# Stacked q and k of groups 1 to 7 laid out by DMA through DRAM instead of by matmul, in a one-core attention and expert kernel

## The chip, the cores and the metric

One core of a Trainium2 chip (trn2) runs the program. The metric is the device time of one execution in microseconds (us). Engines are named as in the profile: PE is TensorE, PEld its weight load, DVE VectorE, ACT ScalarE, POOL GpSimd, and SP SyncE, which here only issues DMAs. SPq is SP's sequencer, where a DMA is issued.

## What is computed

Two sequences of 512 tokens with 128 features, 16 heads of 8 features. The reference, cut to what matters here:

```python
x = x + attn(cond(x, c, w_cond), w_qkv, w_out)
# attn: q, k, v per head (B=2, H=16, S=512, hd=8), rotary turn of q and k
scores = einsum('bhsd,bhtd->bhst', q, k) / sqrt(hd)      # causal
attn   = softmax(scores);  out = einsum('bhst,bhtd->bhsd', attn, v) @ w_out.T
x = x + ffn(cond2(x, ...))   # cond2: 2 shared and 8 routed experts; ffn: top 3 of 8 zones per sequence
```

The softmax subtracts each row's true maximum. All is in fp32, and the score products are made exact to fp32 level by splitting q and k into a high and a low part.

## The kernel before, in words

The 32 pairs of sequence and head are worked in 8 groups of 4 heads (`GROUPS` = 8, `NG` = 4 groups to a sequence, `HG` = 4 heads to a group). After the rotary turn, `qk_hi` and `qk_lo` hold the high and low parts of q (index 0) and k (index 1), with 128 partitions = 16 heads x 8 features. A group's score matmuls want another layout, `stacked[:, 2n + i, :]`: each of the 4 heads takes 32 partitions, made of four blocks of 8 rows. For q the blocks are (ones or maximum rows, hi, hi, lo), for k (ones, hi, lo, hi). One product of K = 32 rows then sums hi*hi + hi*lo + lo*hi.

Before, `stack(w)` builds this on PE: for each group and for q and k, one matmul of a 0/1 selection matrix `sel` with `qk_hi` and one with `qk_lo` (L1254, L1255), into a PSUM bank; ACT's `copy_stacked(w)` (L926 for q, L928 for k, which adds the ones rows as a bias) moves it to SBUF. Group 0 has its own first version in halves (`stack_half`, `place_q0`, `copy_k0`, `copy_q0`).

Then, for each group n:

- SP's `pad_q(n)` and `pad_k(n)` copy each head's 32 partitions from `stacked` into the zeroed buffers `q_pad` and `k_pad` (4 DMAs each), so that a matmul over 128 partitions sees one head alone. Two buffers of each are used in turn.
- `scores_for_max(n, u)`, 12 units (L1271): PE makes q x k for the maximum, in a ring of three PSUM banks. DVE's `reduce_max` (L617) masks and reduces each block. `place_max` (L630, L632) puts the negated maxima into `max_pad`, and `lay_max_under_q` (L1283, L1285) adds them to q's free rows; ACT copies the result (`copy_qm`, L945).
- `scores_for_exp(n, u)`, 6 units (L1302, L1305, L1306): PE makes k x q, in two pairs of PSUM banks used in turn (`ST_ORDER`), ACT takes the exponential (L939), POOL masks the diagonal (L515).
- `weigh_v` (L1322): PE multiplies with v; ACT copies out (L951); SP's `store_sums(n)` writes it to DRAM.

Each engine runs a fixed list; waits are semaphores. PE's list is the loop at the end of its block: in iteration n stand the exponential units of group n, the last three blocks of `weigh_v` of group n - 1, and the maximum units of groups n + 1 and n + 2 (they run 20 units ahead, `LEAD`). In iterations 0 to 4 the two `stack` calls of group n + 3 (`STACK_IN`) stand between `scores_for_exp(n, 3)` and `(n, 4)`, and take a turn in the banks of `ST_ORDER`. Groups 1 and 2 are stacked earlier, between the maximum units of group 0. The second sequence's q and k are projected in `project(0)` and `project(1)` and turned by POOL while group 0 runs.

Expert weights (`raw`, 1792 KB) are loaded in one DMA after group 0. ACT and POOL split them in seven chunks into high and low parts (`split_high`, `split_low`), at the places in `SPLITS`; chunk 4 and later overwrite `qk_hi` and `qk_lo`, so they wait for the last `stack`. `INV_AT` says behind which maximum units DVE inverts and normalises the first sequence's sums; for this, SP's `gather(0)` reads sums and outputs back from DRAM, and `spread_inverse(0)` writes and rereads the inverse.

After the attention come experts and zones, a loop that PE fills; nothing in it is touched.

Of the kernel before, what the change touches and what calls it, by code (L numbers as in the profile page):

```python
# [7 lines left out]
ACT = mybir.ActivationFunctionType  # L8
# [97 lines left out]
INV_AT = [78, 88]  # L106
SPLITS = {(2, 0): 0, (2, 2): 1, (3, 0): 2, (3, 2): 3, (4, 0): 4, (4, 2): 5, (5, 0): 6}
# [32 lines left out]
def program(nc, io, scratch, out):  # L140
# [9 lines left out]
    with ctx:  # L150
# [120 lines left out]
        def sum_of(i):  # L271
# [86 lines left out]
        def _(sp):  # L358
# [11 lines left out]
            def pad_q(n):  # L370

                s = n % 2
                sp.wait_ge(rep_copied, 3 if n == 1 else 2 * n + 3)
                if n >= 2:
                    sp.wait_ge(mx_full, (n - 1) * MXU)
                for j in range(HG):
                    q = slice(32 * j, 32 * j + 32)
                    sp.dma_start(f32_of(q_pad[s][q, j, :]), f32_of(stacked[q, 2 * n, :])).then_inc(q_padded[s], 16)

            def pad_k(n):  # L380

# [12 lines left out]

# [32 lines left out]
            pad_q(2)  # L427
# [33 lines left out]
        def _(pool):  # L461
# [5 lines left out]
            G.memset(f32_of(sel[:, 1, :, :]), 0.0).then_inc(sel_zero, 1)  # L467
# [5 lines left out]
            for g in range(2, NG):  # L473
                G.memset(f32_of(sel[:, g, :, :]), 0.0).then_inc(sel_zero, 1)
# [8 lines left out]
            def split_low(k):  # L483
# [3 lines left out]
                if k == UP_COLS // S:  # L487
                    pool.wait_ge(rep_ready, 2 * GROUPS + 2)
# [20 lines left out]
            for n in range(GROUPS):  # L509
                for c in range(3):  # L510
# [344 lines left out]
        def _(act):  # L855
# [797 lines left out]
```

## Time and profile before

| | |
|---|---|
| median of 3 runs | 205.31 us (204.97 to 205.75) |
| profiled execution | 205.4 us, of which the core's span is 203.7 us |
| PE busy | 187.9 us, 92% of the span |
| ACT busy | 147.7 us, 73% |
| DVE busy | 141.5 us, 69% |
| attention loop (first exponential unit to the last group's value matmuls) | about 29 to 107 us |
| DMA | 15.72 MB, mean 77 GB/s |

A busy share is an average over stages. What an edit is worth is read from the rows of its stage: which engine stood idle, and who released it.

### The profile page before, as it was taken

Reading aid. Unit: us, or ns where it says so; the run is one execution under the profiler, and the core shown is the slowest. Engines: PE = TensorE matmul, PEld = TensorE weight load, DVE = VectorE, ACT = ScalarE, POOL = GpSimd, SP = SyncE. Lnnn points to the kernel's source line nnn. Section 1 sums busy time; section 2 is a strip of 40 time slices with the busy share of each in tenths; the row PEclk is TensorE's granted clock in tenths of the full one; section 3 lists DMA queues with packets and bytes.
Section 4 is the critical chain, followed back from the end, with each engine's and each line's share of the span. In section 5 each row is a group of like instructions: output and inputs, shape, how many; then the busy total and the mean of one; then the engine's idle time right before and its main releaser. Section 6 shows DMA issues by size and latency. Waiting matters only on the chain.

```text
span 203.7 us, 3373 instructions
## 1 busy us (share of the span) xinstructions
PE 187.9 (92%) x1034; PEld 131.2 (64%) x1034; DVE 141.5 (69%) x459; ACT 147.7 (73%) x245; POOL 85.1 (42%) x100
## 2 busy tenths in 40 slices
PE   7994999999999997998999999999799989999993
PEld 3753766666666663664466776776557857788881
DVE  4584689888888885898027798468979845566552
ACT  4487848677878776879774485465688899899980
POOL 4616068461336363743332261021356962198000
PEclk9999799999999999999999999999999999999999
DMA  5602321229633233332111199600000000001001
GB/s 155 219 0 52 101 67 41 53 52 316 215 91 88 70 102 91 83 103 72 34 52 45 37 326 340 169 0 0 0 3 2 0 0 0 2 3 52 0 0 52
DMA packets 9509, 15.72 MB, mean 77 GB/s; under 512 B 2116, under 2 KB 3268, under 8 KB 9364
## 3 DMA queue, kind: packets, MB, share of 16 engines
q1 hardware_dynamic: 8916, 15.12, 24.5%
q10 hardware_dynamic: 576, 0.39, 0.6%
q8 instruction: 8, 0.13, 0.3%
q14 instruction: 9, 0.07, 0.1%
HBM read 9.16 MB, written 2.42 MB: 57 GB/s over the span
## 4 chain that ended last, share of the span: by engine, by line
PE 68%; DVE 15%; ACT 11%; issue 4%; POOL 1%; DVEq 0%; ACTq 0%; POOLq 0%
PE psum L1271 10%; PE psum L1400 9%; PE psum L1322 8%; PE psum L1402 8%; PE psum L1401 8%; PE psum L1302 6%; DVE psum L617 3%; PE psum L1305 2%; PE psum L1194 2%; PE psum L1254 2%; PE psum L1139 2%; DVE t_raw L763 2%; PE psum L1306 1%; ACT t_q_pad L991 1%; PE psum L1255 1%
## 5 line engine op out<-in xcount | busy, mean ns | idle before, releaser
L617 DVE CUSTOM_DVE_ANT_0 psum<-psum,t_causal 128x128 f32<-128x128 f32 (+3 forms) x128 | 59.5, 523 | 15.5 <-PE psum L1271 14.9
L939 ACT ACTIVATE t_probs<-psum 128x768 f32<-128x768 f32 (+1 forms) x48 | 41.3, 883 | 4.0 <-PE psum L1302 3.0
L1271 PE MATMUL psum<-t_stacked,t_q_pad 128*128 128x256 f32 (+2 forms) x128 | 36.9, 361 | 0.6 <-ACT t_q_pad L886 0.2
L515 POOL TENSOR_SCALAR_AFFINE_SELECT t_probs<-t_probs 128x512 f32<-128x512 f32 x32 | 20.0, 638 | 32.4 <-ACT t_probs L939 32.4
L1271 PEld LDWEIGHTS psum<-t_stacked,t_q_pad 128*128 128x128 f32 x128 | 22.0, 190 | 13.8 <-DVE t_row_max L617 9.8
L781 DVE SCALAR_TENSOR_TENSOR t_q_pad<-psum,t_zw_all,t_q_pad 128x512 fp32r<-128x512 f32 x24 | 17.9, 749 | 11.6 <-ACT t_q_pad L989 11.6
L975 ACT ACTIVATE t_raw<-psum 128x512 f32<-128x512 f32 x24 | 14.3, 595 | 10.4 <-PE psum L1446 7.7
L1322 PE MATMUL psum<-t_probs,t_v_all 128*32 128x512 f32 (+3 forms) x256 | 20.5, 439 | 0.0
L549 POOL TENSOR_TENSOR t_q_pad<-t_raw,t_q_pad 128x512 fp32r<-128x512 f32 x8 | 10.3, 1290 | 20.1 <-ACT t_q_pad L991 20.1
L1302 PE MATMUL psum<-t_q_mov,t_k_pad 128*128 128x512 f32 (+1 forms) x64 | 18.3, 371 | 0.2
L617 DVE DVE_READ_ACCUMULATOR2_ANT t_row_max<- 128x1 f32 x128 | 18.2, 142 | 0.0
L989 ACT ACTIVATE t_q_pad<-psum,t_zw_all 128x512 fp32r<-128x512 f32 x24 | 16.6, 690 | 1.9 <-PE psum L1402 1.5
L769 DVE TENSOR_TENSOR psum<-t_raw,psum 128x512 f32<-128x512 f32 x16 | 11.1, 692 | 7.8 <-ACT t_raw L975 7.8
L1400 PE MATMUL psum<-t_stacked,t_up_hi 128*128 128x512 f32 x32 | 14.0, 437 | 0.7 <-DVE t_q_pad L784 0.4
L975 ACT ACTIVATE psum<-psum 128x512 f32<-128x512 f32 x24 | 14.1, 586 | 0.3 <-PE psum L1402 0.3
L1401 PE MATMUL psum<-t_stacked,t_up_lo 128*128 128x512 f32 x32 | 12.6, 394 | 0.0
L1402 PE MATMUL psum<-t_stacked,t_up_hi 128*128 128x512 f32 x32 | 12.6, 393 | 0.0
L1302 PEld LDWEIGHTS psum<-t_q_mov,t_k_pad 128*128 128x128 f32 x64 | 11.2, 189 | 1.8 <-ACT t_probs L939 0.7
L784 DVE TENSOR_TENSOR t_q_pad<-psum,t_q_pad 128x512 fp32r<-128x512 f32 x16 | 10.9, 684 | 2.0 <-ACT t_q_pad L991 1.6
L1322 PEld LDWEIGHTS psum<-t_probs,t_v_all 128*32 128x32 f32 x256 | 6.6, 109 | 8.4 <-issue 3.9
L1305 PE MATMUL psum<-t_q_mov,t_k_pad 128*128 128x256 f32 x32 | 9.1, 307 | 2.0 <-ACT t_probs L939 2.0
L945 ACT CAST t_q_mov<-psum 128x512 fp32r<-128x512 f32 x8 | 4.7, 586 | 8.0 <-PE psum L1285 8.0
(236 smaller groups left out, 420.9 us busy)
## 6 DMA issues: line engine op xcount, KB each, us to landing
t_k_pad<-t_stacked SPq DMA_DIRECT2D x32, 64.0 KB, 2.0
t_probs<-in_L_ffn_Wa SPq DMA_DIRECT2D x2, 1024.0 KB, 8.7
t_q_pad<-t_stacked SPq DMA_DIRECT2D x28, 64.0 KB, 2.0
scratch<-t_o_sb SPq DMA_DIRECT2D x7, 256.0 KB, 2.0
t_raw<-in_experts SPq DMA_DIRECT2D x1, 1792.0 KB, 7.6
t_raw<-in_rotary SPq DMA_DIRECT2D x2, 256.0 KB, 4.9
out_dram<-t_probs SPq DMA_DIRECT2D x2, 256.0 KB, 2.0
t_raw<-in_w_all ACTq DMA_DIRECT2D x2, 128.0 KB, 3.0
```

The lines of the kernel that those rows point to most:

```text
L515: last = G.affine_select(out=tri, in_=tri, compare_op=ALU.is_ge, fill=0.0, base=0, pattern=[[0, HG], [1, P]], channel_multiplier=-1)
L617: last = V.tensor_tensor_reduce(scores, scores, causal[:, S - width:S], 1.0, 3 * BIG, ALU.add, ALU.max, row_max[s][:, qb, j:j + 1])
L781: V.scalar_tensor_tensor(h_lo[r], hidden_of(i), weight_of(i), f32_of(h_hi[r]), ALU.mult, ALU.subtract).then_inc(lo_done, 1)
L939: A.activation(probs[s][:, c, 2 * h2:2 * h2 + 2, 0:w], ST[:, slot_of("exp", n, u):slot_of("exp", n, u) + 2, 0:w], ACT.Exp, scale=float(1.0 ...
L975: A.activation(o, pair_of(i)[:, 0, :], func, scale=scale).then_inc(act_done, 1)
L989: A.activation(h_hi[r], hidden_of(i), ACT.Identity, scale=weight_of(i)).then_inc(hi_done, 1)
L1271: last = T.matmul(ring("max", n, u)[:, i * 2 * P:i * 2 * P + width], q_pad[s][:, j, qb * P:(qb + 1) * P], stacked[:, 2 * n + 1, 0:width], ...
L1302: last = T.matmul(bank[:, 0:S - c * P], k_pad[s][:, j, c * P:(c + 1) * P], q[:, c * P:S], start=True, stop=True)
L1322: last = T.matmul(PV[32 * j:32 * j + 32, lo:hi], v_all[:, v0:v0 + 32], probs[n % 2][:, c, j, o:o + hi - lo], start=(kb == 0 and lo == 0), ...
L1400: T.matmul(o, hi, x_hi, start=start, stop=False)
L1401: T.matmul(o, lo, x_hi, start=False, stop=False)
L1402: return T.matmul(o, hi, x_lo, start=False, stop=stop)
```

## The change

Groups 1 to 7 are no longer stacked by `stack` and `copy_stacked`; both functions go, with three of the four selection matrices. Instead SP writes the rows of `qk_hi` and `qk_lo` to a DRAM area that has the stacked layout (`spill`: per sequence and per q or k, three DMAs: hi twice, lo once), fills in the ones and zero rows once from an input (`spill_rest`), and reads whole groups back into `stacked` (`load_stacked`). `pad_q` (groups 1 to 7) and `pad_k` read that DRAM area as well, not `stacked`. The two bank pairs of `ST_ORDER` carry only projections and exponential units. `raw` is loaded in seven DMAs, spread over iterations 1 to 4. The chunks are split one iteration later, and DVE's inversion and normalisation stand 2 and 5 maximum units later.

```diff
-STACK_IN = {0: 3, 1: 4, 2: 5, 3: 6, 4: 7}
-ST_ORDER = [("stack", 2), ("project", 1)]
+BY_PE = 1
+SPILLS = 3
+ST_ORDER = [("project", 0), ("project", 1)]
 for _n in range(GROUPS):
-    ST_ORDER += [("exp", _n, _u) for _u in range(4)] + ([("stack", STACK_IN[_n])] if _n in STACK_IN else [])
-    ST_ORDER += [("exp", _n, 4), ("exp", _n, 5)]
+    ST_ORDER += [("exp", _n, _u) for _u in range(STU)]
...
-INV_AT = [78, 88]
-SPLITS = {(2, 0): 0, (2, 2): 1, (3, 0): 2, (3, 2): 3, (4, 0): 4, (4, 2): 5, (5, 0): 6}
+INV_AT = [80, 93]
+SPLITS = {(3, 0): 0, (3, 2): 1, (4, 0): 2, (4, 2): 3, (5, 0): 4, (5, 2): 5, (6, 0): 6}
+EXPERT_LOADS = [(), (0, 1), (2, 3), (4, 5), (6,), (), (), ()]
...
             def pad_q(n):
                 s = n % 2
-                sp.wait_ge(rep_copied, 3 if n == 1 else 2 * n + 3)
                 if n >= 2:
                     sp.wait_ge(mx_full, (n - 1) * MXU)
                 for j in range(HG):
                     q = slice(32 * j, 32 * j + 32)
-                    sp.dma_start(f32_of(q_pad[s][q, j, :]), f32_of(stacked[q, 2 * n, :])).then_inc(q_padded[s], 16)
+                    sp.dma_start(f32_of(q_pad[s][q, j, :]), laid(n, 0)[q, :]).then_inc(q_padded[s], 16)
...
+            def spill(b, i):
+                q = slice(0, P) if b else slice(32 * BY_PE, P)
+                sp.wait_ge(hi_ready, 4 * b + (i + 1 if b else 3 + i))
+                for r in ((1, 2), (1, 3))[i]:
+                    sp.dma_start(laid_blocks(b, i)[r], f32_of(qk_hi[q, i, :])).then_inc(spilled[i], 16)
+                sp.wait_ge(lo_ready, 4 * b + (i + 1 if b else 3 + i))
+                sp.dma_start(laid_blocks(b, i)[(3, 2)[i]], f32_of(qk_lo[q, i, :])).then_inc(spilled[i], 16)
...
+            def load_stacked_part(n, i):
+                sp.dma_start(f32_of(stacked[:, 2 * n + i, :]), laid(n, i)).then_inc(ld_stack[n], 16)
...
+            spill_rest()
+            spill(0, 0)
+            spill(0, 1)
+            sp.wait_ge(rest_rows, 16 * 2)
+            sp.wait_ge(spilled[0], 16 * SPILLS)
+            sp.wait_ge(pad1_zero, 1)
+            pad_q(1)
+            sp.wait_ge(spilled[1], 16 * SPILLS)
+            load_stacked(1)
             sp.wait_ge(pads_zero, 1)
             pad_k(0)
...
             for n in range(GROUPS):
+                if n == 1:
+                    for written in spilled:
+                        sp.wait_ge(written, 2 * 16 * SPILLS)
                 if n + 3 < GROUPS:
+                    load_stacked(n + 3)
                     pad_q(n + 3)
+                if n == 0:
+                    spill(1, 0)
                 if n + 2 < GROUPS:
                     pad_k(n + 2)
+                if n == 0:
+                    spill(1, 1)
...
                 if n < GROUPS - 1:
                     store_sums(n)
-                if n == 0:
-                    sp.wait_ge(v_ready, B)
-                    sp.wait_ge(roped_ready, 6)
-                    sp.dma_start(raw[:], io["experts"]).then_inc(ld_raw, 16)
+                for k in EXPERT_LOADS[n]:
+                    load_experts(k)
                 if n == NG - 1:
                     gather(0)
...
             def split_high(k):
                 hi, lo, c, at_ = chunks[k]
-                if k == 0:
-                    act.wait_ge(ld_raw, 16)
+                act.wait_ge(ld_raw[k], 16)
                 if k == UP_COLS // S:
-                    act.wait_ge(rep_ready, 2 * GROUPS + 2)
+                    for written in spilled:
+                        act.wait_ge(written, 2 * 16 * SPILLS)
...
                 elif u == 0:
                     pe.wait_ge(q_padded[s], 16 * HG * ((n + 1) // 2))
-                    pe.wait_ge(rep_copied, 4 if n == 1 else 2 * n + 4)
+                    pe.wait_ge(ld_stack[n], 16 * 2)
...
             for u in range(1, MXU):
                 scores_for_max(0, u)
-                if u == 4:
-                    stack(2)
-                    stack(3)
                 if u == 6:
                     project_v(0)
-                if u == 8:
-                    stack(4)
-                    stack(5)
             project(1)
```

What PE has in a row between the maximum units of group 0 (L1271 before, L1291 after; L1254 and L1255 are `stack`, L1218 and L1259 the value projection, L1208 and L1249 `project(1)`). Before:

```order
L1271 MATMUL psum<-t_stacked,t_q_pad 128x384
L1254 MATMUL psum<-t_dn_hi,t_sel 128x512
L1255 MATMUL psum<-t_dn_lo,t_sel 128x512
L1254 MATMUL psum<-t_dn_hi,t_sel 128x512
L1255 MATMUL psum<-t_dn_lo,t_sel 128x512
L1271 MATMUL psum<-t_stacked,t_q_pad 128x384 x2
L1218 MATMUL psum<-t_raw 128x128 x4
```

After, with the semaphores waited for in brackets:

```order
L1291 MATMUL psum<-t_stacked,t_q_pad 128x384 [waits mx_reduced,rep_copied,q0_placed]
L1291 MATMUL psum<-t_stacked,t_q_pad 128x384 [waits mx_reduced,q0_placed] x2
L1259 MATMUL psum<-t_raw 128x128 [waits ld_wv,mx_reduced,xc_ready1,xc_ready0]
L1259 MATMUL psum<-t_raw 128x128 x3
L1291 MATMUL psum<-t_stacked,t_q_pad 128x384 [waits mx_reduced,q0_placed]
L1291 MATMUL psum<-t_stacked,t_q_pad 128x512 [waits mx_reduced]
L1291 MATMUL psum<-t_stacked,t_q_pad 128x512 [waits v_copied]
L1291 MATMUL psum<-t_stacked,t_q_pad 128x512 [waits mx_reduced] x2
L1249 MATMUL psum<-t_raw 128x512 [waits rep_copied,q0_placed,xc_ready2]
L1249 MATMUL psum<-t_raw 128x512
L1291 MATMUL psum<-t_stacked,t_q_pad 128x256 [waits mx_reduced,ld_stack1,q_padded1]
```

The stacks are gone from between the units, and the first unit of group 1 now waits for DMAs alone.

SP's first DMAs after the inputs. Before (L388 is `pad_k`, L378 `pad_q`):

```order
L388 DMA t_k_pad<-t_stacked 32x512 [waits rep_copied,pads_zero]
L388 DMA t_k_pad<-t_stacked 32x512 x3
L378 DMA t_q_pad<-t_stacked 32x512 [waits rep_copied,pad1_zero]
L378 DMA t_q_pad<-t_stacked 32x512 x3
L424 DMA t_small<-in_small 128x365
```

After (L410 and L412 are `spill`, L391 `pad_q`, L430 `load_stacked`, L403 `pad_k`):

```order
L420 DMA scratch<-in_rest 28x4096 x2
L410 DMA scratch<-t_dn_hi 12x8x512 [waits hi_ready]
L410 DMA scratch<-t_dn_hi 12x8x512
L412 DMA scratch<-t_dn_lo 12x8x512 [waits lo_ready]
L410 DMA scratch<-t_dn_hi 12x8x512 [waits hi_ready]
L410 DMA scratch<-t_dn_hi 12x8x512
L412 DMA scratch<-t_dn_lo 12x8x512 [waits lo_ready]
L391 DMA t_q_pad<-scratch 32x512 [waits pad1_zero,spilled_q,rest_rows]
L391 DMA t_q_pad<-scratch 32x512 x3
L430 DMA t_stacked<-scratch 128x512 [waits spilled_k]
L430 DMA t_stacked<-scratch 128x512
L403 DMA t_k_pad<-t_stacked 32x512 [waits rep_copied,pads_zero]
```

`pad_k(0)`, first before, now stands behind 14 other DMAs.

## Rows read from the trace of the kernel before

**Rows 1.** Windows from one group's weigh_v to the next, groups 1 to 6
```profile
43.19:52.88 9.69, 9.69 (x78) 6.64 (x81) 8.17 (x35) 7.72 (x12) 3.68 (x5) 1.00 0.71 244
52.88:62.80 9.92, 9.90 (x77) 6.55 (x81) 8.18 (x35) 7.86 (x12) 3.75 (x6) 1.00 0.36 100
...
72.72:84.28 11.56, 10.14 (x78) 6.57 (x81) 8.40 (x36) 8.47 (x14) 5.17 (x8) 1.00 0.34 97
84.28:93.52 9.24, 9.22 (x73) 5.95 (x77) 8.59 (x38) 7.11 (x10) 5.66 (x7) 1.00 0.32 90
```
**Rows 2.** Timeline: the stall in group 4, and group 5's first maximum after weigh_v
```profile
76.41 0.40 PE L1254 MATMUL psum<-t_dn_hi,t_sel 128*128 128x512 f32 x1
76.64 0.39 PE L1255 MATMUL psum<-t_dn_lo,t_sel 128*128 128x512 f32 x1
...
77.07 0.62 ACT L1034 CAST t_dn_hi<-t_raw 128x512 fp32r<-128x512 f32 x1 [1.28 <-PE psum L1255]
...
78.45 0.38 PE L1305 MATMUL psum<-t_q_mov,t_k_pad 128*128 128x256 f32 x1 [1.42 <-ACT t_probs L939]
...
86.33 0.40 PE L1271 MATMUL psum<-t_stacked,t_q_pad 128*128 128x256 f32 x2
```
**Rows 3.** Windows: busy us of each engine, clock granted to PE, DMA
```profile
16.00:18.00 2.00, 0.44 (x1) 0.19 (x1) 1.73 (x10) 1.88 (x8) 2.00 (x3) 1.00 0.20 49
...
20.00:22.00 2.00, 2.00 (x8) 1.81 (x8) 0.84 (x3) 1.73 (x4) 0.00 (x0) 0.50 0.08 20
```
**Rows 4.** Timeline, 17 to 29 us: start us, us, engine, line, count [idle before <-releaser]
```profile
17.08 0.60 DVE L617 CUSTOM_DVE_ANT_0 psum<-psum,t_causal 128x384 f32<-128x384 f32 x1
...
17.89 1.01 ACT L917 COPY t_probs<-psum 128x1024 f32<-128x1024 f32 x1
...
19.04 0.47 PE L1254 MATMUL psum<-t_dn_hi,t_sel 128*128 128x512 f32 x1 [2.47 <-ACT t_probs L917]
...
21.16 0.57 DVE L617 CUSTOM_DVE_ANT_0 psum<-psum,t_causal 128x384 f32<-128x384 f32 x1 [3.42 <-PE psum L1271]
21.23 1.80 PE L1218 MATMUL psum<-t_raw 128*128 128x128 f32 x8
...
23.07 0.78 ACT L910 COPY t_v_all<-psum 128x128 f32<-128x128 f32 x4 [0.38 <-PE psum L1218]
...
25.40 1.96 PE L1208 MATMUL psum<-t_raw 128*128 128x512 f32 x4 [0.32 <-ACT t_stacked L928]
```
**Rows 5.** Timeline: ACT's high parts, first exponential unit, a later project_v
```profile
13.51 0.41 ACT L876 CAST t_dn_hi<-t_x 128x256 fp32r<-128x256 f32 x1
...
28.98 0.73 PE L1302 MATMUL psum<-t_q_mov,t_k_pad 128*128 128x512 f32 x2
...
38.25 1.13 PE L1218 MATMUL psum<-t_raw 128*128 128x128 f32 x8
```
**Rows 6.** The page: DMA issues, KB each, median us to landing
```profile
scratch<-t_o_sb SPq DMA_DIRECT2D x7, 256.0 KB, 2.0
...
t_small<-in_small SPq DMA_DIRECT2D x1, 182.5 KB, 2.8
```
**Rows 7.** Timeline of SP: DMA issues
```profile
20.64 2.42 SPq L378 DMA_DIRECT2D t_q_pad<-t_stacked  x4
...
25.17 3.88 SPq L378 DMA_DIRECT2D t_q_pad<-t_stacked  x4
...
74.84 0.33 SPq L393 DMA_DIRECT2D scratch<-t_o_sb  x1
77.33 0.59 SPq L402 DMA_DIRECT2D t_sums<-scratch  x1
...
78.90 2.45 SPq L378 DMA_DIRECT2D t_q_pad<-t_stacked  x4
```
**Rows 8.** Line L378 (pad_q): issue ns min/median/max, and landing
```profile
L378 SPq DMA_DIRECT2D t_q_pad<-t_stacked x28: 507/590/2052, 20.6 to 80.8; - x28
...
DMA to landing us min/median/max: 1.9/2.0/5.6
```

More of the change, by code:

```diff
@@ L300, in program @@
         k_padded = [sem(f"k_padded{s}") for s in range(2)]
+        spilled = [sem(f"spilled_{x}") for x in "qk"]
+        ld_stack = {n: sem(f"ld_stack{n}") for n in range(BY_PE, GROUPS)}
         stored = [sem(f"stored{s}") for s in range(2)]
         xc_ready = [sem(f"xc_ready{k}") for k in range(3)]
+        ld_raw = [sem(f"ld_raw{k}") for k in range(len(SPLITS))]
         block = ctx.enter_context(nc.Block())
@@ L346, in hidden_of, with laid, laid_blocks @@
             return pair_of(i)[:, 1, :]
+        def laid(n, i):
+            return scratch[GROUPS + 1 + i * (GROUPS - BY_PE) + n - BY_PE]
+        def laid_blocks(b, i):
+            first = GROUPS + 1 + i * (GROUPS - BY_PE) + (NG - BY_PE if b else 0)
+            slots = scratch[first:first + (NG if b else NG - BY_PE)]
+            return slots.rearrange("g (j r d) t -> r (g j) d t", j=HG, r=KB)
         def slot_of(*item):
@@ L387, in pad_k, with spill_rest, load_stacked @@
                     q = slice(32 * j, 32 * j + 32)
-                    sp.dma_start(f32_of(k_pad[s][q, j, :]), f32_of(stacked[q, 2 * n + 1, :])).then_inc(k_padded[s], 16)
+                    src = f32_of(stacked[q, 2 * n + 1, :]) if n < BY_PE else laid(n, 1)[q, :]
+                    sp.dma_start(f32_of(k_pad[s][q, j, :]), src).then_inc(k_padded[s], 16)
+            def spill(b, i):
[5 more added lines that the diff above has]
+                sp.dma_start(laid_blocks(b, i)[(3, 2)[i]], f32_of(qk_lo[q, i, :])).then_inc(spilled[i], 16)
+            def spill_rest():
+                for i in range(2):
+                    first = GROUPS + 1 + i * (GROUPS - BY_PE)
+                    slots = scratch[first:first + GROUPS - BY_PE]
+                    rows = slots.rearrange("g (j r d) t -> r (g j) d t", j=HG, r=KB)[0]
+                    sp.dma_start(rows, io["rest"][i].unsqueeze(0).broadcast_to(
+                        [(GROUPS - BY_PE) * HG, HD, S])).then_inc(rest_rows, 16)
+            def load_stacked(n):
+                for i in (1, 0):
+                    load_stacked_part(n, i)
+            def load_stacked_part(n, i):
+                sp.dma_start(f32_of(stacked[:, 2 * n + i, :]), laid(n, i)).then_inc(ld_stack[n], 16)
             def store_sums(n):
@@ L915, in copy_projection @@
                 act.wait_ge(qk_ready, 4 + i + 1)
-                at_ = slot_of("project", i) if i else 0
+                at_ = slot_of("project", i)
                 A.copy(unrot[:, 2 * i:2 * i + 2, :], ST[:, at_:at_ + 2, :]).then_inc(pj_copied, 1)
-            def copy_stacked(w):
-                i = w % 2
-                act.wait_ge(rep_ready, w + 3)
-                if w == 3:
-                    act.wait_ge(const_ready, 1)
-                bank = psum[:, (2, 3, 4, 5)[w - 2], :] if w < 6 else ST[:, slot_of("stack", w // 2) + i, :]
-                if i == 0:
-                    A.copy(stacked[:, w, :], bank).then_inc(rep_copied, 1)
-                else:
-                    A.activation(stacked[:, w, :], bank, ACT.Identity, bias=one_col[:]).then_inc(rep_copied, 1)
             def exp(n, u):
@@ L1047, in _ @@
             place_q0(3, 0)
-            take_sel(1)
             copy_k0(1)
```

98 lines of the change are left out of this document (37 added, 61 removed).

## The prediction

> **What bounds the kernel now.** I read the page first, then the timeline of the start, then windows from one group's value matmuls to the next, then the chain of waits and SP's own rows.
>
> In the attention loop PE paces. The windows [rows 1] run from `weigh_v` of one group to that of the next. A group takes 9.69 or 9.92 us (groups 2 and 3 both 9.92) and PE is busy for 9.69 and 9.90 of it, while DVE is busy for 8.17 and ACT for 7.7 to 7.9. Group 5 has no stacks and takes 9.24, with PE busy 9.22. Group 4 takes 11.56 with PE busy only 10.14: here something else stops PE. The timeline shows what [rows 2]: ACT's `split_high(4)` at 77.07 had waited 1.28 us for the last stack (L1255), the exponential behind it was late, and PE's next exponential unit (L1305 at 78.45) sat 1.42 us.
>
> The start is paced by a chain through ACT and PE, not by PE's work. Between 16 and 18 us PE is busy for 0.44 of 2 us [rows 3]. PE's first `stack` (L1254) at 19.04 waited 2.47 us for ACT's copy of the projection (L917, 17.89 to 18.90), since it wants that copy's banks [rows 4]. The maximum units of group 0 stand behind that stack in PE's list, so DVE, done with unit 4 at about 17.7, stood still for 3.42 us until 21.16 [rows 4]. PE also lost its clock: 0.50 was granted from 20 to 22 us, the lower level (1.2 GHz), after that idle stretch [rows 3]. The first exponential unit ran on PE at 28.98 [rows 5].
>
> **The change, part by part.** Sums are against the profiled execution, 205.4 us, of which 203.7 us is span; the median of the runs is 205.31, so 0.1 comes off at the end.
>
> *Start, with data always there.* I replay the order. DVE ends unit 4 at 17.7 and takes at most 0.60 for each of units 5 and 6 [rows 4]: 18.9. `project_v(0)` stands between units 6 and 7 and needs unit 4's bank, so it starts at 17.7. It took 1.80 at the low clock [rows 4] and a later one 1.13 [rows 5]; with 1.5 it ends at 19.2, and unit 7 is reduced by 20.1, unit 8 by 20.75. Unit 9 takes v's bank: ACT, done with its identities at about 17.9, copies the projection (1.01) and two halves of q, is free at about 19.5 and copies v in 0.78 [rows 4], to 20.3. Units 9 to 11 are a little longer, 0.7 each by estimate, and end with the placing of the maxima (0.5, an estimate too) at about 23.2. PE meanwhile ran unit 11 at about 21.2 and needs 1.96 us for `project(1)` [rows 4]: to 23.2. Two units of group 1, the laying of the maxima and ACT's copy of them follow as before, some 1.8 us by estimate, and the first exponential unit is on PE at 25.0 instead of 28.98: **4.0 us** earlier.
>
> *Start, is the data there?* ACT's high half of k starts at 13.51 [rows 5], so q's high part is whole at about 13.1, q's low at 13.6, k's low at 14.4. The six spills at 0.5 us each leave SP from 13.15 to 16.1; q's last one, at 14.2, lands 2.0 later, as a store to DRAM of 256 KB does [rows 6]: 16.7 with its issue. `pad_q(1)`, four issues in 2.4 [rows 7], to 19.1. The two loads of `stacked` to 20.3, landing 2.8 us after issue, as the 182.5 KB of `small` did from DRAM [rows 6]: 22.5. That is 0.7 before 23.2. `pad_k(0)` is issued to 22.7 and landed at 24.3, 0.7 before 25.0. So nothing is lost, but both covers are thin. One issue of `pad_q` took 2.05 in place of 0.59 [rows 8], in the train that took 3.88 [rows 7]; if such a hiccup falls into this train, 1.5 - 0.7 = 0.8 is lost. I take 0.3. The start is worth **-3.7**; bounds: 0 to the bad side if each of the two hops lands at the slowest that L378 shows (5.6, [rows 8]: twice 3.6, less 0.7, is over 4.0), and -5.0 if also the low clock vanishes (0.7 on `project_v` and as much around it). The two `spill_rest` DMAs (0.9 MB) are issued near 5.0 and have until 16.7; I cost them at nothing. If they were 1 us late it would be paid in full.
>
> The Trainium skill (DMA: Bandwidth & Descriptors, "Anatomy of one DMA") says of this sort of detour that the fixed 2 us of a DMA is mostly the wait for the write's receipt and can be surprisingly long when the target is HBM. Here the median store to DRAM landed in 2.0, and pads inside SBUF in 2.0 too [rows 6, 8], so the trace does not show the penalty; by the page the start would shrink and end in my first rival.
>
> *Groups 0 to 3, stacks gone.* A group has four stack matmuls, which start 0.23 apart (76.41 and 76.64 [rows 2]), so 0.92 at most. What it gives is read from group 5, which has all but the stacks: 9.24 against 9.69, 9.92 and 9.92 [rows 1], that is 0.45 + 0.68 + 0.68 = **-1.8**. Bounds: 0 if DVE or ACT takes over, -2.8 for three times 0.92. Group 0 I leave at nothing: there DVE, one unit after the other, covers the stack (if not, up to -0.9 more).
>
> *Group 4.* 11.56 falls to 9.24 [rows 1], since ACT's chunk 4 moves to group 5 and waits for stores that landed some 40 us before: **-2.3**. Bounds: -1.3 (ACT's wait alone) and -2.6.
>
> *ACT.* Seven pairs of copies go; they are inside the numbers above. The splits move on by one group. The one that comes into group 6 (0.6) stands behind the exponential that PE waits for: nothing.
>
> *SP and the pads.* Per group SP issues 2.4 + 2.4 for pads, 1.2 for two loads, 0.4 for the store, 0.9 for two weight loads: 7.3 of 9.24 us. `pad_q(n + 3)` waits for DVE's last group and stands behind `store_sums(n - 1)`, which is free 2.1 after `weigh_v` (74.84 against 72.72 [rows 1, 7]). So it is issued from 4.6 to 7.0 after `weigh_v` of group n and landed by 8.9; group n + 2's first maximum wants it one period later, at 9.24 + 2.05 = 11.3 (86.33 against 84.28 [rows 1, 2]). Cover 2.4. For group 7 it is thin: `gather(0)` comes in between. Its store takes 2.5 from issue to the gather's first DMA (74.84 to 77.33), the gather 1.57 (to 78.90), the pads 2.45 [rows 7]. With two weight loads and two more loads of 0.6, and these hidden in part by the 2.5, the last pad is issued at 9.3 and lands at 11.3: no cover at all. I take **+0.3**, bounds 0 and +1.5. Nothing stands behind it in SP's list that is wanted earlier than 1 us after it comes; `normalise(0)` moved 5 units on covers the later gather.
>
> *Weight loads.* Each chunk (256 KB) is issued several us before its split; a load of 182.5 KB lands in 2.8 [rows 6]. Nothing; if not covered, up to 2.8 per chunk.
>
> After the loop nothing changes, so what the loop gains is kept: PE fills that stage from a fixed list.
>
> Sum: -3.7 - 1.8 - 2.3 + 0.3 = -7.5. 205.4 - 7.5 = 197.9, less 0.1: **197.8 us**.
>
> **The rivals.**
>
> *The DMA route is late at the start.* If each of the two hops takes 1 to 2 us more than 2.0, the 4.0 shrinks by 2 x 1 - 0.7 = 1.3 up to 3.3, and group 7's pads cost up to 2: 199.1 to 203; the middle is 201. For it: covers of 0.7, and one landing of 5.6 among 28 [rows 8]. Against it: medians of 2.0 for 64 and 256 KB.
>
> *More comes off.* The clock stays at 2.4 GHz through the start (-1.0), groups lose the full 0.92 (-1.0 in sum) and group 0 also gains 0.5: 195.3. For it: PE is idle for less time before `project_v`, and ACT is lighter in groups 1 and 2. Against it: group 5 shows what a group without stacks takes.
>
> *Slower: q's pads starve PE in each group.* The place is SP's list. If reads from DRAM land e later than 2.0, the start loses 2e - 0.7, group 7 e, and groups 4 to 6 what e is over 2.4. At e = 2.3 the gain of 7.5 is nearly gone (2 x 2.3 - 0.7 + 2.3 = 6.2); at e = 3.6, the slowest landing in the trace [rows 8], it costs 6.5 + 3.6 + 3 x 1.2 = 13.7: 211. Against it: DMA engines are busy for 0.32 to 0.36 of the time in those groups (0.71 in group 1, while the expert weights load) [rows 1], before some 0.5 MB more per group.
>
> *No change.* The stacks' time was covered, DVE (8.2 of 9.9 [rows 1]) paces once they are gone, and the DMAs eat what the start gives: 204.3 to 206.3. The 3.42 and 1.42 us of plain waiting [rows 2, 4] speak against it.
>
> **How the numbers follow.** Forecast (196.3 to 199.4): 0.50. Late start (199.4 to 203): 0.23. More comes off (194.5 to 196.3): 0.15. No change: 0.04. Slower: 0.08. A measurement of this kernel can tell 0.5%, 1.0 us, from no change. The range 195.0 to 202.0 leaves out the no-change and slower cases (0.12) and the ends of two others (some 0.08). Faster by over 0.5%: 0.50 + 0.23 + 0.15 = 0.88; within: 0.04; slower: 0.08.
>
> **What the profile of the changed kernel would show.** Right: DVE's idle time of 3.42 before a three-block unit gone, the first exponential unit on PE at 25 to 26, and its wait, if any, put down to `q_pad`, `stacked` or `k_pad` DMAs by under 1 us; windows of 9.1 to 9.4 from `weigh_v` to `weigh_v` in groups 1 to 5, group 4 among them; the loop's end near 100. Wrong: PE's first unit of group 1, or the first exponential unit, idle for over 1.5 us behind a DMA; a gap in front of the first maximum unit of groups 4 to 7; windows that stay at 9.7 with DVE above 95% busy; or ACT waiting for `ld_raw`.

## The result and the profile after

The changed kernel takes 197.57 us in the median (197.07 to 198.35, 4 runs) beside 205.39 of the kernel before: ratio 0.962, 95% interval 0.959 to 0.966, so 7.8 us or 3.8% faster. The profiled execution took 197.56 us, with a span of 195.8. In a few executions of some kernels the chip was in a slower state with a lower granted clock; the medians and ratios in this document leave these out.

The page of the changed kernel, the lines that answer to the table of before (packets, MB and rate are of all DMA):

```profile
span 195.8 us, 3320 instructions
PE 180.1 (92%) x1006; PEld 124.1 (63%) x1006; DVE 143.7 (73%) x459; ACT 137.9 (70%) x228; POOL 83.6 (43%) x97
DMA packets 13985, 23.06 MB, mean 118 GB/s; under 512 B 2632, under 2 KB 3784, under 8 KB 13912
```

PE's busy time fell by 7.8 us and keeps its share of 92%: in the loop it still paces. DMA moves 23.06 MB instead of 15.72.

Windows of the changed kernel from one group's `weigh_v` to the next, groups 1 to 6; columns as in [rows 1]:

```profile
40.24:49.23 8.99, 8.99 (x74) 5.95 (x77) 8.06 (x35) 6.65 (x10) 3.67 (x5) 1.00 0.65 203
49.23:58.19 8.96, 8.96 (x74) 5.95 (x77) 8.06 (x35) 6.29 (x9) 2.50 (x5) 1.00 0.74 220
58.19:67.15 8.96, 8.96 (x73) 5.85 (x77) 8.05 (x35) 6.77 (x10) 3.71 (x6) 1.00 0.71 211
67.15:76.09 8.94, 8.94 (x73) 5.93 (x77) 8.05 (x35) 7.06 (x11) 4.95 (x7) 1.00 0.66 188
76.09:85.55 9.46, 8.84 (x74) 5.77 (x77) 8.59 (x36) 7.29 (x11) 5.85 (x8) 1.00 0.57 169
```

Four windows of 8.94 to 8.99 us in which PE is busy from end to end, against 9.69, 9.92, 9.92 and 11.56 [rows 1]; then one of 9.46 with 0.6 of idle PE. The first exponential unit and that idle stretch in PE's timeline of the changed kernel:

```profile
24.18 0.71 PE L1291 MATMUL psum<-t_stacked,t_q_pad 128*128 128x256 f32 x4 [1.71 <-issue]
26.04 0.73 PE L1322 MATMUL psum<-t_q_mov,t_k_pad 128*128 128x512 f32 x2
...
78.93 0.51 PE L1291 MATMUL psum<-t_stacked,t_q_pad 128*128 128x256 f32 x2 [0.62 <-DMA t_q_pad<-scratch]
```

And SP's timeline of the changed kernel, with the first two DMAs of `gather(0)` and what came behind them:

```profile
71.33 0.61 SPq L452 DMA_DIRECT2D t_sums<-scratch  x1
71.99 0.59 SPq L457 DMA_DIRECT2D t_packed_out<-scratch  x1
72.63 1.06 SPq L430 DMA_DIRECT2D t_stacked<-scratch  x2
73.73 1.82 SPq L391 DMA_DIRECT2D t_q_pad<-scratch  x4
```

The start gained 28.98 - 26.04 = 2.94 us [rows 5], and PE waited 1.71 us before group 1's first maximum. The view names no releaser for this wait ("issue"); in PE's list the unit waits there for group 1's pads of q and its two loads of `stacked`, and a_kfirst below shows that it was the loads. At 78.93 PE waits for group 7's pads, which SP issued behind `gather(0)`.

What the start gained it gained in the chain that the forecast named. DVE and PE between the maximum units of group 0, in the timeline of the changed kernel:

```profile
17.59 1.13 PE L1259 MATMUL psum<-t_raw 128*128 128x128 f32 x8
18.93 0.57 DVE L680 CUSTOM_DVE_ANT_0 psum<-psum,t_causal 128x384 f32<-128x384 f32 x1 [0.46 <-PE psum L1291]
```

DVE stands for 0.46 us where it stood for 3.42 [rows 4], and `project_v` takes 1.13 us instead of 1.80: PE's granted clock stayed at 1.00, the upper level, through this start.

The account, by the first matmul of each group's last `weigh_v` blocks: start -2.94, group 0 nothing (14.14 us before, 14.13 after), groups 1 to 3 -0.70, -0.96 and -0.96, group 4 -2.62, group 5 +0.22, group 6 +0.13. That is -7.83, and the first expert matmul moved from 107.82 to 99.98, -7.84. After it nothing moved against it.

SP's first DMAs after the inputs, in the timeline of the changed kernel:

```profile
12.81 1.60 SPq L410 DMA_DIRECT2D scratch<-t_dn_hi  x2
14.45 0.74 SPq L412 DMA_DIRECT2D scratch<-t_dn_lo  x1
15.24 1.53 SPq L410 DMA_DIRECT2D scratch<-t_dn_hi  x2
16.81 0.75 SPq L412 DMA_DIRECT2D scratch<-t_dn_lo  x1
17.85 1.75 SPq L391 DMA_DIRECT2D t_q_pad<-scratch  x4
20.30 0.82 SPq L430 DMA_DIRECT2D t_stacked<-scratch  x2
21.22 2.52 SPq L403 DMA_DIRECT2D t_k_pad<-t_stacked  x4
```

The landings of three kinds, from the page's DMA issues of the changed kernel:

```profile
t_stacked<-scratch SPq DMA_DIRECT2D x14, 256.0 KB, 3.6
t_q_pad<-scratch SPq DMA_DIRECT2D x28, 64.0 KB, 3.2
t_k_pad<-scratch SPq DMA_DIRECT2D x28, 64.0 KB, 2.2
```

The six spills took 0.74 to 0.79 us each to issue, not 0.5. The pads of q were all issued by 19.60, but SP stood until 20.30 for k's last spill, which so landed 3.5 us after its issue began at 16.81, not 2.5 (2.0 and an issue of 0.5). The loads of `stacked` land in 3.6 us in the median, not 2.8.

### The profile page after: what moved, and what is told of

The parts are those of the page before. It is cut to its first block, busy times and chain, and to the rows that moved or that the text cites. A ratio compares the mean times of both kernels' runs of the same rounds, so it can differ in the third digit from the quotient of the medians.

```text
span 195.8 us, 3320 instructions
## 1 busy us (share of the span) xinstructions
PE 180.1 (92%) x1006; PEld 124.1 (63%) x1006; DVE 143.7 (73%) x459; ACT 137.9 (70%) x228; POOL 83.6 (43%) x97
## 2 busy tenths in 40 slices
DMA packets 13985, 23.06 MB, mean 118 GB/s; under 512 B 2632, under 2 KB 3784, under 8 KB 13912
## 4 chain that ended last, share of the span: by engine, by line
PE 61%; DVE 15%; ACT 11%; issue 6%; DMA 3%; SPq 2%; POOL 1%; DVEq 0%; ACTq 0%; POOLq 0%
PE psum L1414 9%; PE psum L1291 8%; PE psum L1416 8%; PE psum L1415 8%; PE psum L1342 7%; PE psum L1322 5%; DVE psum L680 3%; DMA t_q_pad<-scratch 2%; PE psum L1235 2%; PE psum L1249 2%; PE psum L1181 2%; DVE t_raw L826 2%; PE psum L1325 2%; ACT t_q_pad L1044 1%; DVE t_raw L830 1%
## 5 line engine op out<-in xcount | busy, mean ns | idle before, releaser
L1291 PE MATMUL psum<-t_stacked,t_q_pad 128*128 128x256 f32 (+2 forms) x128 | 37.3, 361 | 3.9 <-issue 1.7
L1291 PEld LDWEIGHTS psum<-t_stacked,t_q_pad 128*128 128x128 f32 x128 | 21.4, 188 | 18.8 <-DVE t_row_max L680 10.8
L1414 PE MATMUL psum<-t_q_pad,t_dn_hi 128*128 128x512 f32 x24 | 9.8, 406 | 0.5 <-POOL t_q_pad L612 0.4
```

Source lines behind the costliest of these rows:

```text
L1291: last = T.matmul(ring("max", n, u)[:, i * 2 * P:i * 2 * P + width], q_pad[s][:, j, qb * P:(qb + 1) * P], stacked[:, 2 * n + 1, 0:width], ...
L1414: T.matmul(o, hi, x_hi, start=start, stop=False)
```

## The experiments

The theory: three savings that add up (the start's chain through ACT and PE; PE's time for the stacks; ACT's wait for the last stack in group 4), less two waits for DMAs (group 1's load, group 7's pads). Ratios are against the kernel before, beside it on the same chip. "First exponential" is the start of the first exponential unit on PE; it and the windows are of one profiled execution each.

| run | median us | ratio (95%) | first exponential | windows, groups 1 to 5 |
|---|---|---|---|---|
| before | 205.39 | 1 | 28.98 | 9.69 9.92 9.92 11.56 9.24 |
| changed | 197.57 | 0.962 (0.959 to 0.966) | 26.04 | 8.99 8.96 8.96 8.94 9.46 |
| b_splits | 204.59 | 0.994 (0.991 to 0.996) | 28.97 | 9.69 10.17 9.92 10.16 9.99 |
| b_reuse | 203.62 | 0.986 (0.980 to 0.993) | 28.80 | 8.95 9.41 8.99 9.20 11.54 |
| b_reuse_inv | 199.89 | 0.973 (0.970 to 0.977) | 28.08 | 9.00 9.33 8.96 8.96 8.97 |
| a_pe_work | 199.69 | 0.972 (0.966 to 0.978) | 26.08 | 9.61 9.61 9.62 9.62 8.95 |
| a_act_work | 197.08 | 0.959 (0.954 to 0.964) | 25.67 | 8.99 8.97 8.95 8.94 8.98 |
| a_inv | 197.94 | 0.965 (0.961 to 0.969) | 25.46 | 8.97 8.97 8.99 9.20 10.08 |
| a_oneload | 199.66 | 0.972 (0.966 to 0.977) | 26.05 | 9.00 8.96 10.98 8.95 9.46 |
| after_again | 198.11 | 0.963 (0.960 to 0.966) | 26.92 | 8.95 8.99 8.97 8.97 9.30 |
| a_spill16 | 196.99 | 0.959 (0.955 to 0.962) | 25.93 | 8.95 8.96 9.00 8.95 9.14 |
| a_kfirst | 196.99 | 0.958 (0.954 to 0.963) | 25.02 | 8.95 8.97 8.97 8.98 9.47 |
| a_gather | 196.98 | 0.959 (0.956 to 0.963) | 25.67 | 8.95 8.97 8.99 8.95 8.98 |
| a_all | 196.42 | 0.954 (0.951 to 0.957) | 26.92 | 8.95 8.97 8.99 8.95 8.98 |

**b_splits.**
```diff
 # the kernel before
-SPLITS = {(2, 0): 0, (2, 2): 1, (3, 0): 2, (3, 2): 3, (4, 0): 4, (4, 2): 5, (5, 0): 6}
+SPLITS = {(3, 0): 0, (3, 2): 1, (4, 0): 2, (4, 2): 3, (5, 0): 4, (5, 2): 5, (6, 0): 6}
```


> The kernel before with one edit: the seven chunks are split one group later, as in the changed kernel; the stacks stay. My theory: group 4's window was long (11.56 us against 9.92) only because ACT's chunk 4 waited for the last stack, so that window falls to 9.9 and the whole to about 203.7 us (-1.6). Rival: the stall is that of the last stack itself (bank turn, PE order) and stays: under 0.5 us off.

Group 4's window fell from 11.56 to 10.16, so ACT's wait for the last stack was what made it long. But group 5's rose from 9.24 to 9.99. DVE's timeline in b_splits says why:

```profile
90.12 0.69 DVE L645 TENSOR_TENSOR t_packed_out<-t_packed_out,t_packed_sum 128x512 f32<-128x512 f32 x1 [0.61 <-DMA t_packed_sum<-scratch]
```

`normalise(0)`, at unit 88, had to wait for the round trip of the inverse through DRAM: with group 4 shorter, DVE came there sooner than the DMA. Half of group 4's gain was given back at once. The ratio of 0.994 is 1.3 us (0.7 to 1.9) off, near the 1.6 of the theory; the windows of the one profiled execution add up to only 0.4 off, and no run explains the difference.

**a_pe_work.**
```diff
 # the changed kernel
                 maximum(6)
+                if n < 5:
+                    wait_slot("exp", n, 4)
+                    for i in range(4):
+                        T.matmul(ST[:, slot_of("exp", n, 4) + i // 2, :], stacked[:, 0, 0:P],
+                                 stacked[:, 1, :], start=i % 2 == 0, stop=i % 2 == 1)
                 scores_for_exp(n, 4)
```


> The changed kernel with PE's stack time put back: in groups 0 to 4 four dummy matmuls of 512 columns, in the place of the stacks and into the banks that the next exponential unit overwrites. No copy on ACT, no wait. My theory: PE paces the loop, so windows 1 to 4 go from 8.96 back to 9.9 and the whole up by 3.7 us (group 0 nothing), to 201.3. Rival: the loop gained because ACT was relieved and a turn of the banks went, so the dummies cost under 1.5 us.

Windows 1 to 4 rose by 0.62 to 0.68 us each, 2.6 in sum and not 3.7: the theory was too high, and its rival (under 1.5) too low. PE's time alone is two thirds of the 0.96 that a group gained, not all. In group 0 the dummies cost nothing (14.15 us from the first exponential unit to `weigh_v`).

**a_act_work.**
```diff
 # the changed kernel (semaphores left out)
                 exp(n, 3)
+                if n < 5:   # into an unused part of sel
+                    A.copy(spare[0], stacked[:, 0, :])
+                    A.activation(spare[1], stacked[:, 1, :], ACT.Identity, bias=one_col[:])
```


> The changed kernel with ACT's stack copies put back: in groups 0 to 4 two copies of 512 columns into an unused buffer, where the copies stood. My theory: ACT has the room (6.3 to 7.1 of 8.96 us busy), so it costs under 0.5 us. Rival (ACT relief is what paid): +2 us or more.

Nothing: windows of 8.94 to 8.99, with ACT busy for 7.43 of 8.97 in group 2. The last third of the 0.96 is not ACT's work by itself. What these two runs don't put back is the link between the two: the copy's wait for the stack, and the turn that the stacks took in the banks. Whether that is the last third is not shown.

**b_reuse and b_reuse_inv.**
```diff
 # the kernel before; waits for stacks of groups 3 to 7 become waits for those of group 2
-STACK_IN = {0: 3, 1: 4, 2: 5, 3: 6, 4: 7}
+STACK_IN = {}
+def kept(n):
+    return n if n < 3 else 1 + n % 2
...
-f32_of(stacked[q, 2 * n, :])).then_inc(q_padded[s], 16)
+f32_of(stacked[q, 2 * kept(n), :])).then_inc(q_padded[s], 16)
...
 # b_reuse_inv, besides
-INV_AT = [78, 88]
+INV_AT = [80, 93]
```


> The kernel before with the stacks and copies of groups 3 to 7 left out; these groups use the stacked q and k of groups 1 and 2 again, so their scores are of other heads (the output is not the reference's). No DMA goes through DRAM. It shows the loop without stacks and without the new traffic. My theory: windows 1 to 4 are 8.96 as in the changed kernel, so the traffic costs the loop nothing, start as before (first exponential unit at 29.0), total -2.6 -2.6 = 200.2 us. If the traffic did cost something the windows are shorter than 8.96, 8.7 or less. If DRAM-fed groups are what saves, the total stays over 203.

> The kernel before with the stacks and copies of groups 3 to 7 left out (these groups use the stacked q and k of groups 1 and 2 again, so scores of other heads and an output that is not the reference's), and INV_AT at 80 and 93. My theory: the 11.54 us window of group 5 without the new INV_AT falls to 9.0 and the whole to about 200.5 us, start as before (28.8). Rival: what held group 5 was something else, and the total stays near 203.6.

b_reuse missed by 3.4 us, and most of it comes from one row of DVE's timeline in b_reuse:

```profile
87.63 0.91 DVE L651 TENSOR_TENSOR t_packed_out<-t_packed_out,t_packed_sum 128x512 f32<-128x512 f32 x1 [1.70 <-DMA t_packed_sum<-scratch]
```

What it did to PE, in PE's timeline of b_reuse:

```profile
89.13 1.02 PE L1277 MATMUL psum<-t_stacked,t_q_pad 128*128 128x512 f32 x2 [1.81 <-DVE t_row_max L623]
```

A window of 11.54, made by a wait that the kernel before does not have. It cost more than itself, since PE's clock fell behind it. Windows of b_reuse:

```profile
90.00:92.00 2.00, 2.00 (x12) 0.77 (x14) 2.00 (x8) 1.02 (x1) 0.20 (x1) 0.60 0.00 0
92.00:94.00 2.00, 2.00 (x21) 0.85 (x14) 0.05 (x1) 0.12 (x1) 0.43 (x1) 0.55 0.00 0
```

The window of group 6, which begins at 91.03, took 8.98 us with this stretch in it, and 7.67 in b_reuse_inv. With the two numbers of `INV_AT` group 5's window is 8.97 and the total 199.89, near the 200.5 of the theory. The window of group 2 stays long in both (9.41 and 9.33): there PE waits 0.56 and 0.49 us for pads of q that SP issued behind the single load of the expert weights (the slowest landed in 7.1 us in b_reuse).

The start of b_reuse_inv is that of the kernel before, and yet its first exponential unit came at 28.08 and not at 28.98 or 28.80 (b_reuse). Its clock stayed up, though PE had waited 2.46 us for ACT's copy as in the others. Window of b_reuse_inv:

```profile
20.00:22.00 2.00, 2.00 (x14) 1.63 (x12) 1.37 (x5) 1.98 (x5) 0.00 (x0) 1.00 0.12 30
```

In the kernel before it is 0.50 there [rows 3]. So 0.7 to 0.9 of the 2.94 us that the start gained is the clock, by this estimate, and not the chain.

The windows of b_reuse_inv (groups 3 and 5), with DMA busy for 0.32 and 0.42 of the time, are those of the changed kernel, where it is 0.57 to 0.74:

```profile
60.62:69.58 8.96, 8.96 (x73) 5.99 (x77) 8.05 (x35) 7.05 (x11) 4.93 (x7) 1.00 0.32 89
78.54:87.51 8.97, 8.97 (x73) 5.96 (x77) 8.45 (x36) 7.05 (x11) 5.83 (x8) 1.00 0.42 113
```

So the new traffic costs PE, DVE and ACT nothing inside the loop, but for the pads that come late (group 7, below).

**a_inv.**
```diff
 # the changed kernel
-INV_AT = [80, 93]
+INV_AT = [78, 88]
```


> The changed kernel with the two numbers of INV_AT put back to 78 and 88, so that DVE inverts and normalises the first sequence's sums 2 and 5 maximum units earlier. My theory after the last runs: with a shorter loop the DRAM round trip of the inverse lands too late for unit 88, DVE stands still in front of the normalisation for 1.5 us or more, and PE with it: total +1.5 to +2.5 us against the changed kernel. Rival (my prediction's view, that these numbers are worth nothing): under 0.5 us.

Window 5 is 10.08 instead of 9.46 and window 4 is 9.20 instead of 8.94, and DVE waits 0.53 us for the inverse, after a start that was 0.58 earlier in this run. The ratios differ by 0.3%, which the intervals don't separate; the windows say 0.6 to 0.9 us, less than expected. The numbers are worth something, but not 1.5 us here. PE's wait for group 7's pads was 0.31 us in this run and not 0.62, so the two waits overlap in part.

**a_oneload.**
```diff
 # the changed kernel
-EXPERT_LOADS = [(), (0, 1), (2, 3), (4, 5), (6,), (), (), ()]
+EXPERT_LOADS = [(), (0,), (), (), (), (), (), ()]
...
-                sp.dma_start(raw[:, c], io["experts"][:, c]).then_inc(ld_raw[k], 16)
+                sp.dma_start(raw[:], io["experts"]).then_inc(ld_raw[0], 16)
```


> The changed kernel with the expert weights in one load of 1792 KB, issued where the first two of the seven stand. My theory: it delays group 5's loads and pads, issued right behind it, by 3 to 5 us over a cover of 2.4, so one window is 1 to 2.5 us longer, the rest unchanged: +1 to +2.5 us. Rival (my prediction's view, that the split is worth nothing): under 0.5 us.

As the theory had it. The window of group 3's `weigh_v` to the next in a_oneload:

```profile
58.22:69.20 10.98, 8.85 (x73) 5.77 (x77) 8.16 (x35) 6.99 (x10) 3.76 (x6) 1.00 0.64 201
```

And PE's timeline of a_oneload in it:

```profile
62.56 0.50 PE L1292 MATMUL psum<-t_stacked,t_q_pad 128*128 128x256 f32 x2 [2.13 <-DMA t_q_pad<-scratch]
```

Group 5's pads, issued from 53.20 on behind the 1792 KB, landed in up to 7.4 us, and PE stood for 2.13. The window is 2.0 us longer than the changed kernel's 8.96, and the ratio is 0.972 beside 0.963 of after_again on the same chip, some 1.7 us. So the seven loads keep 1.7 to 2.0 us of the 7.8.

**after_again.** The changed kernel once more, no edit.

> The changed kernel itself, once more, beside the next three. Both theories: ratio 0.962, about 197.6 us, within 0.4%. Its profile shows how far the start and the wait for group 7's pads move from run to run.

The ratio repeats. The profile, of the slowest of the six executions (199.2 us), shows more: PE's wait before group 1 was 2.11 us this time, and its clock fell behind it. Windows of after_again:

```profile
22.00:24.00 2.00, 0.78 (x2) 0.00 (x0) 0.90 (x4) 1.01 (x1) 0.89 (x1) 1.00 0.92 274
24.00:26.00 2.00, 1.11 (x9) 0.96 (x9) 0.60 (x3) 0.00 (x0) 1.92 (x3) 0.93 0.57 135
26.00:28.00 2.00, 2.00 (x8) 1.40 (x6) 1.51 (x10) 0.59 (x1) 0.95 (x1) 0.50 0.86 288
28.00:30.00 2.00, 1.96 (x9) 1.50 (x7) 1.39 (x7) 1.46 (x2) 0.00 (x0) 0.71 0.51 139
```

PE was busy for 0.78 of 2 us, then came a stretch at 0.50, the lower level. Group 0 then took 15.07 us (26.92 to 41.99), not 14.13: 0.9 us on top of the wait. The profile taken first kept 1.00 throughout with a wait of 1.71 us, though PE was busy for only 0.47 of the 2 us from 22 to 24. The ten executions of the changed kernel fall into two sorts by their mean granted clock: six with 0.997 to 1.00 took 197.07 to 197.58 us, four with 0.989 to 0.991 took 198.35 to 199.20.

**a_kfirst.**
```diff
 # the changed kernel: ld_stack[n] becomes a pair of semaphores, for q and k
-            load_stacked(1)
+            load_stacked_part(1, 1)
             sp.wait_ge(pads_zero, 1)
             pad_k(0)
+            load_stacked_part(1, 0)
...
-                    pe.wait_ge(ld_stack[n], 16 * 2)
+                    pe.wait_ge(ld_stack[n][1], 16)
```


> The changed kernel with separate semaphores for the q and the k part of a stacked group: the first maximum unit waits for k alone, and group 1's q part is loaded only behind pad_k(0). My theory: the 1.71 us wait of PE before group 1's first unit was for the last of these loads; with half the bytes in front k lands about 0.5 to 1 us sooner and the total falls by as much, until pad_k(0) is the next to be late. Rival: the wait is for the pads of q or for the spill of k, and nothing changes (under 0.2 us).

**a_spill16.**
```diff
 # the changed kernel, the DRAM area sized for all groups
-                q = slice(0, P) if b else slice(32 * BY_PE, P)
+                q = slice(0, P)
```


> The changed kernel with all four groups of the first sequence in the spills (128 rows in 16 heads, not 96 rows in 12): a third more bytes, but a DMA of the shape whose issue took 0.52 to 0.67 us later on instead of 0.74 to 0.80. My theory: the start waits for the chain of DMAs, so shorter issues (6 x 0.15 to 0.25) bring the first exponential unit from 26.0 to about 25.1 and the total down 0.9 us. Rival: bytes or landing decide, and it is no faster or slower (26.0 to 26.5).

**a_gather.**
```diff
 # the changed kernel
-INV_AT = [80, 93]
+INV_AT = [82, 93]
...
                     pad_q(n + 3)
+                if n == NG:
+                    gather(0)
...
-                if n == NG - 1:
-                    gather(0)
```


> The changed kernel with gather(0) moved behind pad_q(7) in SP's list, and the inversion 2 maximum units later (82). My theory: PE's wait for group 7's pads (0.62 us in the profile of the changed kernel, window 5 of 9.46 us) goes, since those pads no longer stand behind the store's landing and the gather: window 5 at 8.95 to 9.0, total -0.5 us. Rival: the pads are late from DMA traffic, not from their place; or the inverse is now late at unit 82 or 93, and DVE waits: no gain or a loss of up to 1 us.

**a_all.** The last three together.

> The changed kernel with three edits together: spills of all four groups, k's load first with a semaphore of its own, gather(0) behind pad_q(7). My theory: the start gains 1.0 us (k first) and perhaps 0.2 more from the shorter issues, group 7's pads 0.5: about 196.0 us, ratio 0.955. Rival: the edits meet the same wait (pad_k(0) becomes the last), so no more than the 0.6 us that one of them gave.

PE's wait ahead of group 1's first maximum, in the timeline of a_kfirst:

```profile
23.16 0.71 PE L1292 MATMUL psum<-t_stacked,t_q_pad 128*128 128x256 f32 x4 [0.38 <-issue]
```

The same of a_spill16:

```profile
24.04 0.71 PE L1291 MATMUL psum<-t_stacked,t_q_pad 128*128 128x256 f32 x4 [1.10 <-issue]
```

The same of a_gather:

```profile
23.82 0.70 PE L1291 MATMUL psum<-t_stacked,t_q_pad 128*128 128x256 f32 x4 [0.97 <-issue]
```

The same of a_all, and its next wait:

```profile
22.98 0.71 PE L1292 MATMUL psum<-t_stacked,t_q_pad 128*128 128x256 f32 x4 [0.24 <-issue]
26.92 0.71 PE L1325 MATMUL psum<-t_q_mov,t_k_pad 128*128 128x512 f32 x2 [2.14 <-issue]
```

k first takes the wait before group 1 down to 0.38, where the seven profiles with the start of the changed kernel (changed, after_again, a_pe_work, a_act_work, a_inv, a_oneload, a_gather) have 0.97 to 2.11, and the first exponential unit to 25.02, where they have 25.46 to 26.92. Its pads of q and its spills are issued as before, so what the start waited for was this load. Its ratio (0.958) is not separated from that of the changed kernel, and all four of its executions kept a clock of 0.997 or more, which can be a part of the difference.

a_spill16 issues faster (0.61 to 0.71 us each) but its start is within what a repeat moves, 25.93: the theory of 0.9 us failed. SP had issued the last spill by 17.26 us and then still stood for the landings, so that the loads of `stacked` were issued at 20.58 and not earlier than before. The spills took 2.8 to 4.0 us to land in this run.

a_gather's start falls in the same spread although its edit does not touch it. What its edit does show is that group 7's pads are issued earlier, 4.48 us after the first matmul of `weigh_v` and not 6.65 as in the changed kernel (73.73 against 67.08). SP's timeline of a_gather, with `weigh_v` at 66.71:

```profile
71.19 1.82 SPq L391 DMA_DIRECT2D t_q_pad<-scratch  x4
```

SP's timeline of a_act_work, which has the old order, with `weigh_v` at 66.72:

```profile
73.38 1.82 SPq L392 DMA_DIRECT2D t_q_pad<-scratch  x4
```

Its window 5 of 8.98 us without a wait would not prove the cause alone, since a_act_work has 8.98 as well. With the old order the pads were issued at the same place in every run, and PE waited for them 0.62, 0.47, 0.30, 0.31, 0.65, 0.62 us or not at all (changed, after_again, a_spill16, a_inv, a_kfirst, a_oneload, a_act_work): the order leaves no cover, and how long the pads take to land decides. With the new order (a_gather, a_all) they are issued 2.2 us earlier, more than the longest of these waits, and no wait was seen. The ratio, 0.959 beside 0.963, is not separated.

In a_all both waits are small or gone (0.24 and none), and in its profile the next one came: PE stood 2.14 us before the first exponential unit, whose other input is `pad_k(0)`. The slowest pad of k in this run took 4.2 us to land, in the changed kernel 3.5; that it was this one fits the times, but is not shown. That execution took 197.96 us; the median is 196.42, ratio 0.954 (0.951 to 0.957). Beside after_again (0.960 to 0.966) on the same chip it is the version that beats both kernels, by 0.9% over the changed one.

## Why the prediction was right, point by point

- **The total** (197.8 forecast, 197.57 measured) is right because the forecast had the right places of the gain, and by luck in the last microsecond: its terms were off by +0.76 (start), -0.82 (groups 1 to 3), -0.32 (group 4) and +0.05 (pads, with groups 5 and 6), which leaves -0.33. The condition of the first rival, hops of over a microsecond more, came true in part, and so did two conditions of the second (the clock kept at the start in this execution, more per group); they cancelled.
- **Its own signs of being wrong**: one appeared in full, PE's first unit of group 1 idle for 1.71 us behind a DMA (the limit was 1.5), and one in part, a gap in front of the first maximum unit of group 7. The windows of 8.94 to 8.99 and 9.46 lie outside the 9.1 to 9.4 of its signs of being right. DVE's 3.42 gone, the first exponential unit at 26.04 and the loop's end at 99.98 were as it said.
- **The start** was forecast at -3.7 and measured at -2.94. The replay of DVE and PE held: PE was ready for group 1 at 22.47 (24.18 less the 1.71 it waited), 0.7 before the 23.2 of the forecast, for which its clock speaks (`project_v` 1.13 and not 1.5). The step that was off is "is the data there?". The loads of `stacked` were all issued by 21.12, not 20.3: spills at 0.5 to issue took 0.74 to 0.79, and SP then stood 0.7 us for the landing of k's last spill, which the forecast did not cost. It had taken 2.0 for a store to DRAM; the spills took longer to land (3.5 for this one, 2.8 to 4.0 in a_spill16). The load from DRAM then landed in some 3.4, not the 2.8 of one undisturbed load. The cover of 0.7 was gone and another 1 us with it. a_kfirst shows that this load was it. Whether writing to DRAM or the traffic of the other DMAs made the spills land late, no run separates.
- **Groups 1 to 3** were forecast at -1.8 and gave -2.62. The proxy was at fault: group 5 of the kernel before has no stacks, but it has the normalisation. b_reuse_inv, which has it one window later, and the changed kernel show what a clean group takes, 8.96, not 9.24. a_pe_work gives PE's time 0.65 of the 0.96 per group. The bound of -2.8 was nearer.
- **Group 0**, left at nothing: 14.14 before and 14.13 after. Right, and a_pe_work shows the same with the stacks' time put back.
- **Group 4**: -2.3 forecast, -2.62 measured, same proxy. b_splits shows the mechanism.
- **ACT** had room, as argued: a_act_work.
- **SP and the pads**: +0.3 forecast for group 7; PE waited 0 to 0.65 us for them, and 0.62 in the profile above. "No cover at all" was right, but by two errors: the last pad was issued by 8.5 us after `weigh_v`, not 9.3, and it landed some 3.8 after its issue began, not 2.0. The cover of 2.4 for the other groups held: no window shows a wait.
- **`INV_AT` at nothing** was wrong in kind. The forecast read the two numbers as cover for a later gather; they keep DVE from arriving before the inverse once the loop is shorter. Undone, they cost 0.6 to 0.9 us here by the windows, and in b_reuse some 2.7 us by the ratios, a part of which is the clock that PE lost behind the wait.
- **Weight loads at nothing** holds for the seven, but the forecast did not say that the single load would have cost 1.7 to 2.0 us with DRAM-fed groups behind it: the stated cover was of the split, and not of the pads queued behind the load.
- **No change after the loop**: -7.84 at its end, -7.84 in the whole.

## What to carry to other kernels

Speeding up a stage moves every consumer nearer to its DMAs: look for round trips whose cover was the time that you take out, and move their places with it. A proxy for "the same stage without the work" must be searched for other work that only it carries. When a matmul is traded for a trip through DRAM, cost each hop with its issue, its landing behind the traffic that the change itself adds, and the next transfer in line; inside a loop with 2 us of cover it is free, at the start it is on the path. And one profile is one execution: a wait that comes and goes between runs of the same order says how thin a cover is, and an edit is judged by what it moved in the list as well as by the wait that is gone.

## What the runs showed of the hardware

- DMAs from 96 rows in 12 heads took 0.74 to 0.79 us to issue, those from 128 rows in 16 heads 0.61 to 0.71 in their place (a_spill16), though they move a third more bytes.
- These spills to DRAM took 2.8 to 4.0 us to land (a_spill16), where the stores of `o_sb` of 256 KB took 2.0 [rows 6].
- 64 KB pads read from DRAM took 0.42 us to issue, where the same pads read from SBUF had taken 0.59 [rows 8]; they landed in 2.2 (k) and 3.2 (q) instead of 2.0 in the median.
- 64 KB pads issued behind a load of 1792 KB took up to 7.4 us to land (a_oneload).
- The length of a wait did not decide whether PE's clock fell. It fell to 0.50 after waits of 2.47 us (before) and 2.11 (after_again), and to 0.60 and 0.55 in the mean of two windows after 1.81 (b_reuse); it stayed at 1.00 after waits of 2.46 (b_reuse_inv), 2.14 (a_all) and 1.71 (changed). A fall at the start went with 0.7 to 0.9 us more, and the four executions of the changed kernel with a mean clock of 0.989 to 0.991 are the slow end of its spread of 197.1 to 199.2 us.
